# First attention of a pre-norm layer: softmax sums inverted once on 128x8 through DRAM, side items at other steps, one more add on GpSimd

## What is computed

```python
x = x + attn1(layernorm(x))     # 2048 tokens x 128, 16 heads of 64
x = x + ffn(layernorm(x))       # 16 heads of 8, then 4 experts of 512 by a router
# attn1:
q, k, v = split(x @ W_qkv + b_qkv); k = k + pos_enc
scores = q @ k.T / 8;  attn = softmax(scores);  out = (attn @ v) @ W_out + b_out
```

## Time and profile before

| | |
|---|---|
| median of 3 runs | 2182.4 us (2181.78 to 2187.36) |
| profiled execution | 2193.95 us, span 2192.2, clock 0.972 |
| PE busy | 2096.7 us, 96% |
| DVE busy | 1791.5 us, 82% |
| ACT busy | 1703.2 us, 78% |
| POOL busy | 1250.8 us, 57% |
| first attention | about 60 to 1360 us |

### The profile page before, as it was taken

The page is one execution under the profiler, slowest core; times in us unless marked ns, Lnnn a source line. Parts: engine busy times, 40 slices in busy tenths (PEclk is TensorE's granted clock), DMA queues, the critical chain, the costliest instruction groups (busy, mean ns, idle before and its releaser), DMA issues.

```text
span 2192.2 us, 35559 instructions
## 1 busy us (share of the span) xinstructions
PE 2096.7 (96%) x12010; PEld 936.0 (43%) x12010; DVE 1791.5 (82%) x2828; ACT 1703.2 (78%) x2298; POOL 1250.8 (57%) x763
## 2 busy tenths in 40 slices
PE   6999999999999999999999989999999999999997
PEld 3544445445444444444444433333333333333334
DVE  7788888888888888888888857789999999999803
ACT  1688888888888888888888884387888878888862
POOL 1687786886986877877877796331042033025003
PEclk9899999999999999999999998599999999999978
DMA  4000000000000000000000000000000000000000
GB/s 122 20 11 20 11 14 17 10 20 10 11 20 11 19 12 11 20 11 11 20 10 19 31 11 1 1 1 1 1 1 1 2 6 1 2 2 6 2 1 10
DMA packets 18476, 28.05 MB, mean 13 GB/s; under 512 B 2680, under 2 KB 13568, under 8 KB 18176
## 3 DMA queue, kind: packets, MB, share of 16 engines
q1 hardware_dynamic: 18304, 25.79, 3.6%
HBM read 24.47 MB, written 1.18 MB: 12 GB/s over the span
## 4 chain that ended last, share of the span: by engine, by line
PE 69%; DVE 18%; ACT 6%; issue 4%; POOL 3%; DMA 0%; DVEq 0%; POOLq 0%; ACTq 0%
PE acc_o L524 14%; PE acc_o L644 11%; PE scores L502 10%; PE scores L630 10%; PE ring L477 7%; DVE mxp L1323 6%; DVE accp L1359 6%; DVE mxp L1434 3%; ACT prob L826 2%; PE ring L689 2%; POOL accp L990 2%; ACT prob L848 2%; PE ring L697 2%; PE ring L610 2%; PE ring L454 2%
## 5 line engine op out<-in xcount | busy, mean ns | idle before, releaser
L990 POOL TENSOR_TENSOR accp<-accp,prob 128x1024 f32<-128x1024 f32 x318 | 804.9, 2531 | 50.6 <-ACT prob L826 7.1
L1323 DVE TENSOR_REDUCE mxp<-ring 128x1 f32<-128x512 f32 x1024 | 650.3, 681 | 176.9 <-PE ring L477 163.6
L826 ACT ACTIVATE prob<-scores 128x1024 f32<-128x1024 f32 x512 | 519.5, 1015 | 189.3 <-PE scores L502 169.0
L848 ACT ACTIVATE prob<-scores 128x512 f32<-128x512 f32 x1024 | 544.3, 599 | 145.0 <-PE scores L630 142.5
L1434 DVE TENSOR_REDUCE mxp<-ring 128x1 f32<-128x512 f32 x789 | 510.5, 683 | 56.5 <-PE ring L610 40.6
L502 PE MATMUL scores<-q_all,k_all 64*128 64x512 f32 x3072 | 544.6, 408 | 6.5 <-ACT scores L833 3.1
L833 ACT ACTIVATE scores<-minus_all 128x1024 f32<-128x1024 f32 x510 | 524.4, 1028 | 24.1 <-ACT prob L826 0.8
L524 PE MATMUL acc_o<-prob,v 128*64 128x512 f32 x2048 | 497.6, 606 | 0.0
L477 PE MATMUL ring<-k_all,q_all 64*128 64x512 f32 x1024 | 396.8, 436 | 22.4 <-DVE mxp L1323 18.6
L502 PEld LDWEIGHTS scores<-q_all,k_all 64*128 64x128 f32 x3072 | 336.7, 186 | 86.4 <-ACT scores L833 41.2
L630 PE MATMUL scores<-q_all,k_all 32*128 32x512 f32 x1024 | 307.3, 500 | 13.5 <-ACT prob L848 9.2
(11 more groups left out here) (186 smaller groups left out, 1618.4 us busy)
## 6 DMA issues: line engine op xcount, KB each, us to landing
minus_all<-m_dram SPq DMA_DIRECT2D x32, 512.0 KB, 3.6
w_all<-w_pairs SPq DMA_DIRECT2D x1, 1344.0 KB, 10.7
x<-x SPq DMA_DIRECT2D x4, 256.0 KB, 3.6
pos_sb<-pos SPq DMA_DIRECT2D x1, 1024.0 KB, 8.1
w_sb<-w SPq DMA_DIRECT2D x4, 256.0 KB, 4.5
w_all<-w SPq DMA_DIRECT2D x1, 1024.0 KB, 8.4
q_all<-m_rows SPq DMA_DIRECT2D x64, 2.0 KB
out<-ff SPq DMA_DIRECT2D x4, 256.0 KB, 2.3
```

The costliest lines, as they stand in the source:

```text
L826: nc.scalar.activation(prob[:, T % SLOTS1, :, :], sc[T % 2][:, :, :], ACT.Exp, scale=SCALE1).then_inc(exp_done, 1)
L848: nc.scalar.activation(prob2[:, h // 2, T % 2, h % 2, :], sc2[place % 3], ACT.Exp, scale=SCALE2).then_inc(exp2_done, 1)
L990: nc.gpsimd.tensor_tensor(accp[:, k % 2], accp[:, k % 2], prob[:, T % SLOTS1], ALU.add).then_inc(pool_acc, 1)
L1323: done(nc.vector.reduce_max(mxp1[k % 2][:, h * QT + q, kc:kc + 1], bank[:], AX.X), ("max", k, q, kc, h))
```

## The change

The reciprocals of 128x512 a chunk become one of 128x8: the two heads' rows of sums are written to DRAM, read back as 128x8, inverted, written to DRAM and broadcast to 64 partitions each (chunks 0 to 29; chunk 30 keeps the quarters). The side items of a step are dealt out otherwise: K or V at steps 0 and 5 instead of 4 and 6, Q at step 4 and for the chunk one later instead of step 1. GpSimd adds tiles 0 to 12, VectorE 13 (step 7), 14 and 15.

```diff
@@ -29,8 +29,8 @@
 STEPS1 = NT // 2
 SCALE1 = D1 ** -0.5
 SLOTS1 = 8
-POOL_ADDS = 11
-DVE_ADDS = 4
+POOL_ADDS = 12
+DVE_ADDS = 3
 LAST_POOL_ADDS = 9
 LAST_DVE_ADDS = 5
 
@@ -59,14 +59,14 @@
 def last_item1(k, j):
 
     c = k % NC
-    if k == 0 and j in (0, 2, 5):
-        return {0: ("V", 0, 2), 2: ("rows",), 5: ("V", 0, 3)}[j]
-    if j == 1 and k + 2 < CHUNKS1:
-        return ("Q", k + 2)
+    if k == 0 and j in (0, 1, 2, 5, 6, 7):
+        return {0: ("V", 0, 2), 1: ("Q", 2), 2: ("rows",), 5: ("K", 1, 0), 6: ("V", 0, 3), 7: ("K", 1, 1)}[j]
+    if j == 4 and k + 3 < CHUNKS1:
+        return ("Q", k + 3)
     if j == (2 if k < LAST1 else 1) and k > 0:
         return ("sums", k - 1)
-    if j in (4, 6) and k // NC + 1 < PAIRS:
-        half = 0 if j == 4 else 1
+    if j in (0, 5) and k // NC + 1 < PAIRS:
+        half = 0 if j == 0 else 1
         return ("K", k // NC + 1, 2 * c + half) if c < 2 else ("V", k // NC + 1, 2 * (c - 2) + half)
     if j == 3 and k + 1 < CHUNKS1:
         return ("fin", k + 1)
@@ -75,10 +75,13 @@
     return None
 
 
-def recip_quarters(k, j):
-
-    if k < LAST1:
-        return {3: [0], 4: [1], 5: [2, 3]}.get(j, [])
+
+
+ROWS1 = CHUNKS1 - 2
+
+
+def recip_quarters(j):
+
     return {2: [0, 1], 3: [2, 3]}.get(j, [])
 
 
@@ -293,6 +296,8 @@
         oraw = sb("oraw", [128, 2, CW])
         ssum = sb("ssum", [128, CW])
         rec = sb("rec", [128, CW])
+        sums8 = sb("sums8", [128, 2 * CW // 128])
+        rec8 = sb("rec8", [128, 2 * CW // 128])
         onorm = sb("onorm", [128, CW])
         kf = sb("kf", [128, CW])
         w_all = sb("w_all", [128, PAIRS, 384])
@@ -367,6 +372,8 @@
         seeded = sem("seeded")
         pool_acc, dve_acc = sem("pool_acc"), sem("dve_acc")
         rec_ready, onorm_ready, row_ready = sem("rec_ready"), sem("onorm_ready"), sem("row_ready")
+        sums_out, sums_in, rec8_ready = sem("sums_out"), sem("sums_in"), sem("rec8_ready")
+        rec_out, rec_spread = sem("rec_out"), sem("rec_spread")
         mx_ready, m_row, m_out, m_spread = sem("mx_ready"), sem("m_row"), sem("m_out"), sem("m_spread")
         qh_ready, kh_ready, kl_ready = sem("qh_ready"), sem("kh_ready"), sem("kl_ready")
         blank = sem("blank")
@@ -407,6 +414,8 @@
 
         order2 = [it for it in USES if it[0] in ("K2", "Q2")]
 
+        sums_dram = nc.dram_tensor("sums_dram", [2, CW], F32, kind="Internal").ap()
+        rec_dram = nc.dram_tensor("rec_dram", [2, CW], F32, kind="Internal").ap()
         m_dram = nc.dram_tensor("m_dram", [2, 2 * CW], F32, kind="Internal").ap()
 
         block = ctx.enter_context(nc.Block())
@@ -811,7 +820,7 @@
             def sums_copy(k):
                 wait_full(act, ("sums", k))
                 if k > 0:
-                    act.wait_ge(rec_ready, QT * k)
+                    act.wait_ge(sums_out, 16 * k)
                 nc.scalar.activation(ssum[:], ring[bank_of(("sums", k))][:], ACT.Copy).then_inc(free[bank_of(("sums", k))], 1)
 
             def exps(T):
@@ -991,7 +1000,10 @@
 
             def normalise(k):
                 pool.wait_ge(o_copied, k + 1)
-                pool.wait_ge(rec_ready, QT * (k + 1))
+                if k < ROWS1:
+                    pool.wait_ge(rec_spread, 32 * (k + 1))
+                else:
+                    pool.wait_ge(rec_ready, QT)
                 if k > 0:
                     wait_full(pool, ("y", k - 1))
                 nc.gpsimd.tensor_tensor(onorm[:], oraw[:, 0, :], rec[:], ALU.mult).then_inc(onorm_ready, 1)
@@ -1147,8 +1159,8 @@
                         deviations(0, k - CHUNKS1 + 2, stats2, rstd_ready)
                     if t == (POOL_ADDS if k < LAST1 else 6) and k > 0:
                         normalise(k - 1)
-                    if t == 10 and last_item1(k, 4) and last_item1(k, 4)[0] == "K":
-                        split_keys(*last_item1(k, 4)[1:])
+                    if t == 3 and last_item1(k, 0) and last_item1(k, 0)[0] == "K":
+                        split_keys(*last_item1(k, 0)[1:])
                     if t == 8 and k == CHUNKS1 - 2:
                         late(k, 3)
                     if t == 10 and k == CHUNKS1 - 2:
@@ -1159,8 +1171,9 @@
                         late(k, 3)
                     if t == 8 and k == LAST1:
                         deviations(0, 2, stats2, rstd_ready)
-                if last_item1(k, 6) and last_item1(k, 6)[0] == "K":
-                    split_keys(*last_item1(k, 6)[1:])
+                for j in (5, 7):
+                    if last_item1(k, j) and last_item1(k, j)[0] == "K":
+                        split_keys(*last_item1(k, j)[1:])
                 if k == CHUNKS1 - 2:
                     late(k, 6)
             late(LAST1, 5)
@@ -1170,7 +1183,7 @@
             for q in range(QT):
                 cols = slice(q * 128, (q + 1) * 128)
                 if q < QT - 1:
-                    pool.wait_ge(rec_ready, QT * LAST1 + q + 1)
+                    pool.wait_ge(rec_ready, QT + q + 1)
                 else:
                     wait_free(pool, ("sums", LAST1))
                 nc.gpsimd.tensor_tensor(onorm[:, cols], oraw[:, 0, cols], rec[:, cols], ALU.mult).then_inc(onorm_ready, 1)
@@ -1227,7 +1240,32 @@
                 sp.dma_start(w2_sb[:, e], w2[e].rearrange("(f k) n -> k f n", k=128)).then_inc(ld3, 16)
             sp.dma_start(rb_sb[:], router_b[None, :].to_broadcast([128, 1])).then_inc(ld3, 16)
 
+            def sums_rows(k):
+
+                wait_free(sp, ("sums", k))
+                if k > 0:
+                    sp.wait_ge(sums_in, 16 * k)
+                sp.dma_start(sums_dram, ssum[0:128:64, :]).then_inc(sums_out, 16)
+                sp.wait_ge(sums_out, 16 * (k + 1))
+                if k > 0:
+                    sp.wait_ge(rec8_ready, k)
+                sp.dma_start(sums8[:], sums_dram.rearrange("h (a n) -> (h a) n", a=64)).then_inc(sums_in, 16)
+
+            def rec_rows(k):
+
+                sp.wait_ge(rec8_ready, k + 1)
+                if k > 0:
+                    sp.wait_ge(rec_spread, 32 * k)
+                sp.dma_start(rec_dram.rearrange("h (a n) -> (h a) n", a=64), rec8[:]).then_inc(rec_out, 16)
+                sp.wait_ge(rec_out, 16 * (k + 1))
+                if k > 0:
+                    sp.wait_ge(onorm_ready, k)
+                for h in range(2):
+                    sp.dma_start(rec[64 * h:64 * h + 64, :], rec_dram[h:h + 1, :].to_broadcast([64, CW])).then_inc(rec_spread, 16)
+
             for k in range(CHUNKS1):
+                if k >= 2:
+                    sums_rows(k - 2)
                 wait_free(sp, ("fin", k))
                 if k == 0:
                     for h in range(2):
@@ -1239,6 +1277,8 @@
                     sp.wait_ge(seeded, NT * (k - 1) - 2)
                 sp.dma_start(minus_all[:, k % 2].rearrange("p h n -> p (h n)"),
                              m_dram[k % 2:k % 2 + 1, :].to_broadcast([128, 2 * CW])).then_inc(m_spread, 16)
+                if k >= 2:
+                    rec_rows(k - 2)
 
                 if k == CHUNKS1 - 2:
                     wait_full(sp, ("Q", CHUNKS1 - 1))
@@ -1358,10 +1398,16 @@
                     dve.wait_ge(dve_acc, dve_adds(T) - 1)
                 nc.vector.tensor_tensor(accp[:, k % 2], accp[:, k % 2], prob[:, T % SLOTS1], ALU.add).then_inc(dve_acc, 1)
 
-            def reciprocals(k, q):
-                wait_free(dve, ("sums", k))
+            def reciprocals8(k):
+
+                dve.wait_ge(sums_in, 16 * (k + 1))
                 if k > 0:
-                    dve.wait_ge(onorm_ready, k)
+                    dve.wait_ge(rec_out, 16 * k)
+                nc.vector.reciprocal(rec8[:], sums8[:]).then_inc(rec8_ready, 1)
+
+            def reciprocals(q):
+                wait_free(dve, ("sums", LAST1 - 1))
+                dve.wait_ge(onorm_ready, LAST1 - 1)
                 cols = slice(q * 128, (q + 1) * 128)
                 nc.vector.reciprocal(rec[:, cols], ssum[:, cols]).then_inc(rec_ready, 1)
 
@@ -1633,11 +1679,13 @@
                             stats_of(it[1] - CHUNKS1 + NC)
                     if j < 2 and k > 0:
                         add(NT * k - 2 + j)
-                    elif j >= STEPS1 - 2 and k < LAST1:
-                        add(NT * k + NT - 4 + j - (STEPS1 - 2))
-                    if k > 0:
-                        for q in recip_quarters(k, j):
-                            reciprocals(k - 1, q)
+                    elif j == STEPS1 - 1 and k < LAST1:
+                        add(NT * k + NT - 3)
+                    if j == 4 and 0 < k < LAST1:
+                        reciprocals8(k - 1)
+                    if k == LAST1:
+                        for q in recip_quarters(j):
+                            reciprocals(q)
                     if k == LAST1 and j >= 5:
                         if j > 5:
                             add_apart(NT * k + 2 * j)
```

## The result

| | before | changed |
|---|---|---|
| median | 2183.73 us (4 runs) | 2159.61 us (2159.22 to 2160.16, 4 runs) |
| profiled execution | 2193.95, span 2192.2 | 2159.26, span 2157.4 |
| ratio | | 0.989 (0.9878 to 0.9901) |

What follows compares the result with a forecast made beforehand. PE's order of work, broken into by VectorE, was taken to set the time. Gains of 13.7 (keys), 18.9 (V) and 2.0, minus 2.9 and 2.5, made 29 less: 2153 against the median 2182.4; range 2144 to 2187.

Steps and rivals of the forecast that it cites:

- point 4: First attention's chunks: moved side items end VectorE's hold on j=2's last maximum; 38.45 against 39.79, 1.35 less without keys.
- rival A: Chunks without keys: GpSimd comes first, VectorE's add ends at 636.75 as before; 10 less in all, 2172; chance 0.25.
- Rival B: Key chunks: GpSimd becomes the bound at the end of the second split, cycle 40.6; 14 more, 2196; chance 0.12.
- D: Trip through DRAM late by over 2 us; 30 chunks by 0.3 or more each eat the gain; 2190; chance 0.06.
- The 0.3 that I took for that: Key chunks: with one GpSimd add more, the second split ends later and delays the next chunk's first add; up to 0.6.
- point 1: VectorE: four 128x128 reciprocals become one of 128x8, and one add of 1.22 at j=6 goes; nothing counted on the path.
- point 2: SyncE's four small transfers a chunk: reciprocals spread by 656 (653 to 659), y wanted by 660.5; cost nothing.
- point 5: The ends: chunk 0 loses 2.9 (0 to 4) by a late V, chunk 30 2.5 by one add more.
- C: ScalarE's copy at j=0 takes VectorE's place; chunks stay within 0.2 of 39.8; 2182 (2177 to 2188); chance 0.11.

Runs made afterwards that it cites:

- the late ask: The changed kernel with one small unused reduction on VectorE just ahead of its add at j=1 (tile 15), chunks 1 to 29: 2184.65 us, ratio 1.0008.
- the first two experiments: The changed kernel with eleven GpSimd and four VectorE adds again: 2155.31 us; the changed kernel with four reciprocals back and no trip through DRAM: 2158.70 us.
- the run with both ends mended: The changed kernel with chunk 0 dealt out otherwise (K at 4, V 5, K 6, Q 7) and eleven GpSimd adds in chunk 30: 2147.00 us, ratio 0.9839.

## Why the prediction was right, and where it was off

**What bounds, and the item part (point 4): right.** The forecast chunk was 38.45, the measured ones are 38.27 to 38.69 from chunk 3 to 26; chunk 2 gained nothing (39.79, its add took 3.14) and chunk 27 took 37.25. Moving Q away from j=1 lets VectorE ask for its second add before GpSimd's next instruction, and the margin of 0.05 that the rows of before gave was 0.07 in the run. That the moved items carry the gain is shown: alone they give all of it, and without them there is none. That in the chunks without keys it hangs on the order of the two adds is shown too: one instruction of 0.20 us ahead of the ask takes them from 38.3 back to 39.9 to 40.1. In the chunks with keys the order is not the cause, as VectorE comes second there (below); that they gain by VectorE's earlier ask is the reading of the rows, and no run moved Q alone to test it.

The sentence from the Trainium skill on the port pair (SBUF — State Buffer, section SBUF: two separate sides: the first to start holds it for the whole instruction, the other fully blocks) holds in the numbers of both adds, 3.39 and 3.41.

The odds were wrong rather than the sum: I gave rival A, the lost lock, a quarter for a margin of 0.05. In all chunks without keys from 3 to 27 the add took 1.21, and it started 0.06 to 0.08 ahead of GpSimd's: in a repeating chunk the starts repeat to some hundredths, so a margin that small was enough. Rival A's run exists: it is the late ask, and it costs 25 (2184.65 against 2159.61), not the 19 between my two forecasts: a late add in a chunk without keys costs 1.5 to 1.8, where I had 1.35. Its chunks 2 to 27 are 14.1 shorter than before, near the 13x1.05 of rival A; its 2172 fell short by the ends. The chances do not add up either: 0.46 and A without its slow edge make 0.65 for faster, not 0.69, and B and D 0.18 for slower, not 0.14.

**Key chunks: better than forecast, wrong in one piece.** There VectorE lost the race that I had it win; GpSimd's split in chunk 16 starts at 702.50, VectorE's add at 702.60:

```profile
698.33 1.95 DVE L1399 TENSOR_TENSOR accp<-accp,prob 128x1024 f32<-128x1024 f32 x1
...
702.60 2.02 DVE L1399 TENSOR_TENSOR accp<-accp,prob 128x1024 f32<-128x1024 f32 x1
```

```profile
693.33 3.37 POOL L996 TENSOR_TENSOR accp<-prob 128x1024 f32<-128x1024 f32 x1 [3.87 <-ACT prob L835]
...
702.50 1.05 POOL L985 TENSOR_TENSOR k_all<-kf,zero 128x512 fp32r<-128x512 f32 x1
703.62 2.16 POOL L987 TENSOR_TENSOR k_all<-kf,k_all 128x512 fp32r<-128x512 f32 x1
...
728.23 1.28 POOL L1009 TENSOR_TENSOR onorm<-oraw,rec 128x512 f32<-128x512 f32 x1
729.48 1.03 POOL L985 TENSOR_TENSOR k_all<-kf,zero 128x512 fp32r<-128x512 f32 x1
730.59 1.29 POOL L987 TENSOR_TENSOR k_all<-kf,k_all 128x512 fp32r<-128x512 f32 x1
```

```profile
729.79 1.16 PE L552 MATMUL ring<-wout_sb,onorm 128*128 128x128 f32 x8
```

It costs only 2.02, as the split part is short (1.05): the add ends at 704.62, and the scores matmul that stands in front of the next maximum waits for ScalarE's seed until 704.76 anyway. Against the earlier trace rows: from start to the end of normalising GpSimd needs 36.18 (35.9 forecast), and y starts at 729.79, 0.28 after that end at 729.51, without waiting. Rival B was close and did not happen: normalising had 4.02 to spare in the earlier trace rows and has 0.28 now, and in these chunks the first add stands directly behind the second split. The 0.3 that I took for that is about 0.2 in the second key chunk of a pair (38.52 against 38.35) and nothing in the first, so that the twelve key chunks from 4 to 25 gave 1.28 each and not 1.05.

**Reciprocals and VectorE's add (point 1): nothing, right**, shown by the first two experiments. (Four reciprocals are 3.5 by the row of two, 1.75; the 3.7 I wrote is four times the 0.94 of a single one.)

**The trip (point 2): nothing, right.** SyncE's queue in chunk 14:

```profile
632.70 0.50 SPq L1248 DMA_DIRECT2D sums_dram<-ssum  x1
634.28 0.32 SPq L1252 DMA_DIRECT2D sums<-sums_dram  x1
635.40 0.29 SPq L1274 DMA_DIRECT2D m_dram<-m_rows  x1
636.64 0.33 SPq L1278 DMA_DIRECT2D minus_all<-m_dram  x1
641.38 0.32 SPq L1259 DMA_DIRECT2D rec_dram<-rec  x1
642.78 1.10 SPq L1264 DMA_DIRECT2D rec<-rec_dram  x2
```

Sums are on their way at 632.70, sums8 is asked for at 634.28, the inverse leaves at 641.38 and the last broadcast is issued by 643.9; it lands in 2.9. GpSimd's last add ends at 649.7. The slack is 2.9 us where I had counted 0.6: VectorE's turn for the inverse came 20.3 after the chunk's first values (641.16 less 620.88) and not 23, and the broadcast landed 0.7 sooner than the row I took for it.

**The ends (point 5): the term that was mis-sized.** I took 2.9 for chunk 0 and 2.5 for chunk 30, and no cost at all for chunk 1. They cost 5.5, 3.8 and, in chunk 1, 3.2. In chunk 0 and then in chunk 1, PE after:

```profile
96.63 1.94 PE L533 MATMUL acc_o<-prob,v 128*64 128x512 f32 x8
...
104.64 3.33 PE L533 MATMUL acc_o<-prob,v 128*64 128x512 f32 x8 [2.92 <-ACT v L817]
...
151.14 1.38 PE L552 MATMUL ring<-wout_sb,onorm 128*128 128x128 f32 x8 [2.85 <-POOL onorm L1009]
152.44 3.33 PE L533 MATMUL acc_o<-prob,v 128*64 128x512 f32 x8
```

GpSimd's second split of chunk 0 and its first add of chunk 1, then the stretches of the two slow values:

```profile
112.02 1.95 POOL L985 TENSOR_TENSOR k_all<-kf,zero 128x512 fp32r<-128x512 f32 x1 [9.77 <-DVE kf L1357]
...
115.31 2.36 POOL L996 TENSOR_TENSOR accp<-prob 128x1024 f32<-128x1024 f32 x1
```

```profile
104.50:108.00 3.50, 3.36 (x10) 0.94 (x10) 0.00 (x0) 0.00 (x0) 0.00 (x0) 0.57 0.00 0
151.00:155.80 4.80, 4.66 (x18) 1.98 (x18) 1.88 (x2) 0.17 (x1) 4.72 (x3) 0.64 0.02 3
```

PE waits 2.9 us for ScalarE's copy of V, near the 2.4 of the earlier trace rows. What I missed in chunk 0 is what comes behind: the values that follow take 3.33 instead of 1.94, 1.4 more, as the granted clock (third column from the right) is 0.57 in that stretch. With 1.1 for the Q item more these make 5.4 of the 5.5.

Chunk 1, for which I had a gain of 1.05, lost 3.2. Its y waits 2.85 for normalising, and the clock is 0.64 over the values behind. GpSimd is late there: its second K split starts only at 112.02, after 9.77 without work, and its first add of chunk 1 at 115.31, 0.7 before the first values of that chunk (116.00), where in chunk 16 it starts 4.2 before them (693.33 and 697.49). PE's wait for V moves the K item and the start of chunk 1 alike, so that I read this lateness as that of the K item itself, which chunk 0 has at j=7 and the other key chunks have at j=5. This is argued: the run with both ends mended moves V and K together. It gave back 7.8 of the 8.6 of the two chunks (about 1 is the Q item), which shows that chunk 0's order is the cause, and not which of its items.

The late-ask kernel shows what the clock costs in chunk 1: there PE loses its time earlier, behind the late add, y then waits 1.25 only, the values behind take 1.94 at a granted clock of 1.00, and the chunk takes 41.17 instead of 42.84, 1.7 less.

In chunk 30 the values of step 6 and y:

```profile
1261.60 3.42 PE L533 MATMUL acc_o<-prob,v 128*64 128x512 f32 x8
...
1269.74 1.13 PE L552 MATMUL ring<-wout_sb,onorm 128*128 128x128 f32 x8 [2.08 <-POOL onorm L1009]
```

The chunk lost 3.8. The wait is 2.1 as against 1.2 in the earlier trace rows, 0.9 of it; the values at 1261.60 take 3.42 instead of 1.94, 1.5 more, at a granted clock of 0.57 from 1261 to 1265; and PE waits another 1.28 for VectorE ahead of the next chunk's first values. So of the 2.5 that I had put to the add only 0.9 shows as a wait of y, since PE itself comes later by the slow stretch. The clock goes with the add: over chunk 30 it is 0.92 to 0.96 in the six kernels with twelve adds there and 1.00 in the six with eleven. Why it falls is open. Just ahead PE had idled 1.08 and 1.04, but 1.10 and 1.04 in the kernel before as well, where it did not fall.

Chunks 28 and 29 gave 3.1 where I had 2.

Sum against sum: 27 chunks 32.6 forecast and 32.9 measured (36.0-3.2), 28 and 29 2.0 and 3.1, chunks 0 and 30 -5.4 and -9.3; the start and the last chunk, not in the forecast, -0.3. That the 27 chunks hit is partly luck: chunk 1 came 4.2 and chunk 2 1.3 below the forecast, and the other 25 made up for it, with 1.28 instead of 1.05 in the twelve key chunks, 1.51 instead of 1.35 in the twelve from 3 to 26 without keys, and 2.6 in chunk 27. Held apart, the settled chunks 2 to 27 gave 36.0 where 31.5 was forecast, and chunks 0, 1 and 30 cost 12.5 where 4.4 was (5.4 less chunk 1's gain of 1.05); two errors of opposite sign leave 26.4 instead of 29.2.

**Rivals C and D did not happen.** ScalarE's copy at j=0 costs 0.1 (4.00 to 4.06 instead of 3.91). No normalising waited for a broadcast.

## What to carry to other kernels

Look in the steps of a repeating chunk for who is late, and not at who is busy: here 91 us of VectorE's work in 800 could be dropped for no gain, while moving the side items gave all of it. Where VectorE and GpSimd both work on SBUF operands, the order in which they start is a schedule of its own; look which of two adds is asked for first, and know that a few hundredths can decide over some 2 us at VectorE's end. A schedule made for the settled state has to be checked by hand in its first and last chunks, where it cost a third of what it gained.

## What the runs showed that was not expected

- Behind a wait of PE of 2.9 us, in both places where it happened, eight values matmuls took 3.33 instead of 1.94 us, with the granted clock at 0.57 and 0.64 over the stretch (between the full 2.4 GHz and its lower level of 1.2). Behind a wait of 1.25 at the second place they took 1.94 at 1.00. So the stall had a price behind it, 1.4 us in the values alone.
- A VectorE add that starts 0.07 before GpSimd's takes 1.21 and stretches GpSimd's from 2.38 to 3.39; one that starts 0.06 after takes 3.41 and leaves GpSimd's at 2.39. Between the two lies 0.13 us at the start and 2.2 us at VectorE's end.
